# An adaLN block with ProbSparse attention and a soft mixture of experts: the stages of both batches interleaved, and the buffers laid out anew

## The reference

```python
h = layernorm(x) * (1 + ca) + sa                       # per batch
q, k, v = split_heads(h @ Wq + bq), ...(Wk, bk), ...(Wv, bv)
scores = einsum('bhqd,bhkd->bhqk', q, k) * scale
sparsity = scores.max(-1) - scores.mean(-1)
_, top_idx = top_k(sparsity, U)                        # per batch and head
out_sel = softmax(scores_of(q[top_idx], k)) @ v
out = zeros_like(q).at[top_idx].set(out_sel)           # other rows stay zero
x = x + ga * (out @ Wo + bo)
h = layernorm(x) * (1 + cb) + sb
x = x + gb * soft_moe(h)    # rmsnorm, dispatch softmax over tokens, gelu experts, combine softmax
```

## Time and profile before

| | |
|---|---|
| median of 3 runs | 1887.63 us (1884.67 to 1888.17) |
| profiled execution | 1887.74 us, span 1886.0 us, granted TensorE clock 0.913 on average |
| TensorE busy | 1544.0 us, 82% (weight loads 842.5) |
| VectorE busy | 1222.6 us, 65%; 589.6 of it the 512 row maxima L917 |
| ScalarE busy | 1012.3 us, 54% |
| GpSimd busy | 262.8 us, 14% |
| stages of batch 0 | projections 44.10 to 128.70; maxima to 431.20; selection to 485.70; attention to 624.24; output projection and norms to 680; experts and mix to 965.20 |
| stages of batch 1 | projections 965.20 to 1048.60; maxima to 1350.10; selection to 1404.40; attention to 1542.50; the rest to 1886.0 |

### The profile page before, as it was taken

How to read it: one execution, slowest core, us unless ns; L and a number is a source line. 1 busy time by engine, 2 the same in 40 slices (tenths; PEclk the granted TensorE clock), 3 DMA queues, 4 the chain that set the end, 5 groups by cost and what they waited for, 6 DMA issues and landing times.

```text
span 1886.0 us, 29389 instructions
## 1 busy us (share of the span) xinstructions
PE 1544.0 (82%) x8114; PEld 842.5 (45%) x8114; DVE 1222.6 (65%) x3085; ACT 1012.3 (54%) x1342; POOL 262.8 (14%) x294
## 2 busy tenths in 40 slices
PE   2779999993799658898988799999649974979989
PEld 1342222222455423787854222222225533448878
DVE  3539999998777466223134699999977838642211
ACT  1338888882466232433523688888526643333343
POOL 1440000001044200210015100000103440011100
PEclk7879999995799879899998899999859987989989
DMA  9431111121011300243014211112111112004410
GB/s 256 142 97 34 50 34 50 36 65 51 18 53 52 94 1 0 70 148 114 28 47 138 51 43 41 46 38 56 35 44 45 53 41 79 0 14 151 142 39 31
DMA packets 91776, 119.08 MB, mean 63 GB/s; under 512 B 21346, under 2 KB 77378, under 8 KB 91204
## 3 DMA queue, kind: packets, MB, share of 16 engines
q1 hardware_dynamic: 88644, 117.73, 20.9%
q0 software_dynamic: 3072, 0.66, 0.4%
HBM read 93.54 MB, written 24.78 MB: 63 GB/s over the span
## 4 chain that ended last, share of the span: by engine, by line
PE 40%; DVE 34%; issue 13%; ACT 3%; DMA 3%; POOL 3%; SPq 2%; DVEq 1%; PEld 0%; ACTq 0%; PEldq 0%; POOLq 0%
DVE work_area L917 23%; PE psum L1517 6%; PE psum L1564 6%; PE psum L1372 4%; PE psum L1487 4%; PE psum L1395 4%; PE psum L1539 3%; PE psum L1384 3%; PE psum L1525 3%; DVE work_area L947 2%; POOL work_area L486 2%; PE psum L1556 2%; DMA work_area<-q_parts 1%; PE psum L1264 1%; DVE work_area L851 1%
## 5 line engine op out<-in xcount | busy, mean ns | idle before, releaser
L917 DVE CUSTOM_DVE_ANT_0 work_area<-psum,work_area 128x1024 f32<-128x1024 f32 x512 | 589.6, 1220 | 47.6 <-ACT work_area L630 42.7
L630 ACT ACTIVATE work_area<-psum 128x1024 f32<-128x1024 f32 x512 | 510.9, 1027 | 91.2 <-DVE work_area L917 30.6
L1300 PE MATMUL psum<-work_area 96*128 96x512 bf16 x1024 | 311.8, 386 | 47.6 <-DVE work_area L917 7.2
L1290 PE MATMUL psum<-work_area 96*128 96x512 bf16 x1024 | 310.2, 385 | 20.0 <-DMA work_area<-q_parts 14.6
L651 ACT ACTIVATE work_area<-psum 128x614 f32<-128x614 f32 x256 | 164.0, 681 | 80.5 <-PE psum L1384 80.4
L1300 PEld LDWEIGHTS psum<-work_area 96*128 96x128 bf16 x1024 | 64.6, 98 | 266.8 <-DVE work_area L917 249.2
L1290 PEld LDWEIGHTS psum<-work_area 96*128 96x128 bf16 x1024 | 89.7, 98 | 168.8 <-ACT work_area L630 58.2
L1517 PE MATMUL psum<-xn,work_area 128*128 128x257 f32 x512 | 118.8, 391 | 6.3 <-ACT work_area L703 6.3
L990 DVE TENSOR_SCALAR big_area<-iota,rank 128x308 bf16<-128x308 f16 x512 | 122.2, 317 | 0.0
L1487 PE MATMUL psum<-slots_T,work_area 128*128 128x512 f32 x256 | 119.6, 613 | 0.1
L534 POOL DMA_INDIRECT heads_out<-work_area x96 | 99.4, 1036 | 141.2 <-DVE work_area L1019 120.5
(11 more groups left out here) (227 smaller groups left out, 1918.2 us busy)
## 6 DMA issues: line engine op xcount, KB each, us to landing
work_area<-in_L_ffn_w_dram SPq DMA_DIRECT2D x32, 1024.0 KB, 5.2
work_area<-q_parts SPq DMA_DIRECT2D x192, 64.0 KB
k_parts<-work_area SPq DMA_DIRECT2D x24, 384.0 KB, 3.2
work_area<-k_parts SPq DMA_DIRECT2D x32, 192.8 KB
q_parts<-work_area SPq DMA_DIRECT2D x16, 384.0 KB, 2.5
work_area<-q_parts SPq DMA_DIRECT2D x16, 384.0 KB, 5.1
work_area<-k_parts SPq DMA_DIRECT2D x32, 192.0 KB
work_area<-k_parts SPq DMA_DIRECT2D x32, 128.5 KB
```

The costliest lines, as they stand in the source:

```text
L630: s.activation(SC[:, t % 4], PS[:, 2 * (n % 2):2 * (n % 2) + 2].rearrange("p a n -> p (a n)"), ACT.Relu).then_inc(relu_done, 1)
L917: v.tensor_tensor_reduce(SC[:, t % 4], PS[:, 4 + 2 * (t % 2):6 + 2 * (t % 2)].rearrange("p a n -> p (a n)"), SC[:, t % 4], 1.0, -3.0e38, A ...
L1290: last = mm(PS[:, 2 * (n % 2) + k], QS1[par][0:TERMS, t * P:(t + 1) * P], KS[par][0:TERMS, k * 512:(k + 1) * 512], start=True, stop=True)
L1300: last = mm(PS[:, 4 + 2 * (t % 2) + k], QS1[par][0:TERMS, t * P:(t + 1) * P], KS[par][0:TERMS, K1 + k * 512:K1 + (k + 1) * 512], start=Tru ...
```

## The change

The stages of the two batches no longer follow one another: on TensorE, VectorE and ScalarE the order is now projections 0, maxima 0, selection 0 with the projection units of batch 1 in it, attention 0, maxima 1, selection 1 with the value tiles of batch 1 in it, output projection 0, attention 1, experts 0, output projection 1, experts 1. Mean, variance and deviation of batch 1's tokens are formed ahead of maxima 0.

`share(q)` gives the units that round q of the first search carries: one, and two in rounds 3, 7, 11 and 15. TensorE does them behind the natural-order transposes of the round; VectorE does the residual and the cast for `share(q - 1)` between its compares and the wait for the count. GpSimd normalises batch 1's tokens itself. With this go:

- a third residual buffer and a third group buffer `QG` for queries; units use three PSUM banks, natural-order transposes one;
- the next group is turned right behind the first unit of a group; differences are made behind units 0 and 10; the mean key comes at unit 13 (`MEAN_AT`), both in batch 0 as in batch 1;
- keys and queries of the maxima (`KS`, `QS1`) get an area of their own at the end of the working area, which they share with the parts `SPL`, so the first heads are loaded once all parts have been written out; the attention's keys `K2S` lie over the scratch of the search, so their paddings are set behind the ranks (`pads`);
- the SP queue's order, and the search written out instead of looped.

The diff, cut to its core:

```diff
+    MEAN_AT = 13
+    opens = lambda u: u == 0 or UNITS[u - 1][0] < UNITS[u][0]
+    share = lambda q: range(q * NU // ROUNDS, (q + 1) * NU // ROUNDS)
...
         a = Area(work)
-        KS = [a.take([2056], BF16) for _ in range(2)]
-        QS1 = [a.take([L], BF16) for _ in range(2)]
...
-        R1 = a.take([2, GW])
...
+        R1 = a.take([3, GW])
...
+        a = Area(work, parts_at)
+        SPL = a.take([SLOTS, 3, GW], BF16)
+        a = Area(work, parts_at)
+        KS = [a.take([2056], BF16) for _ in range(2)]
+        QS1 = [a.take([L], BF16) for _ in range(2)]
...
+            def first_heads(b):
                 for k in range(SLOTS):
                     sp.wait_ge(parts_out[k], 16 * (NU // SLOTS) * (b + 1))
+                sp.wait_ge(kbar_out, 32 * (b + 1))
+                for par in range(2):
+                    head_to_sbuf(b, 0, par)
...
+            for u in range(NU):
+                parts_to_dram(0, u)
+            first_heads(0)
+            other_heads(0)
+            for g in range(3):
+                queries_to_sbuf(0, g)
+            for u in range(NU):
+                parts_to_dram(1, u)
+                if u == share(G + 1)[-1]:
+                    queries_to_sbuf(0, 3)
+            attention_keys(0)
+            first_heads(1)
+            other_heads(1)
+            for g in range(NG):
+                queries_to_sbuf(1, g)
+            sp.wait_ge(base_ready, 2 * NT + B * H * NT)
+            heads_to_sbuf(0, 0, NT // 4)
+            attention_keys(1)
...
+            def third_part(b, u):
+                pool.wait_ge(part2_ready, b * NU + u + 1)
+                g.tensor_tensor(SPL[:, u % SLOTS, 2], R1[:, u % 3], SPL[:, u % SLOTS, 1], ALU.subtract).then_inc(parts_ready, 1)
+                if u % 10 == 0:
+                    hdiff(b, u // 10)
...
+            def pads(b):
+
                 g.memset(Vh, 0.0).then_inc(pads_ready, 1)
                 g.memset(OS, 1.0).then_inc(pads_ready, 1)
+                pool.wait_ge(rank_ready, b + 1)
+                pool.wait_ge(nm_ready, b + 1)
                 for k in range(2):
                     last = g.memset(K2S[k], 1.0)
...
+            def experts(b):
+
+                for k in range(2):
+                    act.wait_ge(scattered[k], B * PAIRS * CH * 16)
...
+            def residual(b, u):
+
+                g, kind, cc = UNITS[u]
+                dve.wait_ge(part1_ready, b * NU + u + 1)
+                if u > 2:
+                    dve.wait_ge(parts_ready, b * NU + u - 2)
...
+            def split_units(b, units):
+
+                for u in units:
+                    if u == MEAN_AT:
+                        mean_hidden(b)
+                    residual(b, u)
                     if u:
-                        second_part(u - 1)
-                    if u == NU - 2:
-                        mean_key_parts()
-                second_part(NU - 1)
+                        second_part(b, u - 1)
+                    if u == MEAN_AT + 1:
+                        mean_key_parts(b)
...
+                for q in range(ROUNDS):
+                    for k in range(3):
+                        last = v.tensor_scalar(cmpo[:, k], spTf, cand.bitcast(F32)[:, k:k + 1], 0.0, ALU.is_ge, ALU.add, accum_out=cnt[:, k:k + 1])
+                    last.then_inc(cnt_ready, 1)
+                    if b == 0 and q:
+                        split_units(1, share(q - 1))
+                    dve.wait_ge(tot_ready, b * ROUNDS + q + 1)
...
                 v.tensor_scalar(masks[:, 1], spT, thr, None, ALU.is_equal).then_inc(masks_ready, 1)
+                if b == 0:
+                    split_units(1, share(ROUNDS - 1))
+                    second_part(1, NU - 1)
...
+                last.then_inc(qk_ready, 1)
+                if g < NG - 1 and opens(u):
+                    turn_tokens(b, g + 1)
+                if u == MEAN_AT:
+                    mean_key(b)
...
                 for q in range(ROUNDS):
                     pe.wait_ge(cnt_ready, b * ROUNDS + q + 1)
-                    mm(PS[:, 1, 0:3], same_head[:], cnt[:, 0:3], start=True, stop=True).then_inc(tot_ready, 1)
-                    natural(q)
+                    mm(PS[:, 7, 0:3], same_head[:], cnt[:, 0:3], start=True, stop=True).then_inc(tot_ready, 1)
+                    natural(b, q)
+                    if b == 0:
+                        for u in share(q):
+                            unit(1, u)
+                    else:
+                        value_tile(1, q)
...
+            attend(0)
+            maxima(1)
+            select(1)
+            pe.wait_ge(v_copied, B * NT)
+            pe.wait_ge(qn_ready, B * NT)
+            project_heads(0)
+            attend(1)
+            experts(0)
```

624 lines of the change are left out of this document (337 added, 287 removed).

## The result

The changed kernel takes 1820.57 us (median of 4 runs, 1814.84 to 1823.53) against 1887.9 us (four runs of the kernel before; the 1887.63 further up is of three); the ratio is 0.9641 (95% interval 0.9613 to 0.9669), 67 us or 3.6% less. The forecast was 1818 us.

A forecast was written before the change was run, and what follows sets the result against it. The prediction took the serial order of the two batches as the bound, with batch 1's projections (83.4 us) and the threshold searches as thin stages. Terms summed to -69.3 us from 1887.7, so 1818 us; range 1800 to 1840.

The forecast's parts named there:

- (a): Batch 1's projection stage leaves the serial path, its units and value tiles going into the two searches: -83.4 us.
- They just fit: Loads of batch 1's first two heads: issued 17 us before attention 0 ends, such loads taking 14.2 us.
- (b): First search grows by carrying batch 1's 20 units: 79.0 us against 42.7, +36 us.
- The step that rested on a memset's row: First search: VectorE's integer shift waits 0.94 us for the rest of GpSimd's third part, as beside a memset.
- The bound without a waiting shift: First search if no shift waits: rounds of 3.4 and 5.2 us, search growing by about 24 us.
- (c): Batch 0's projections get shorter, mainly since a third residual buffer ends the wait for GpSimd: -11 us, bounds 4 and 15.
- (d): Hand-overs: attention to output projection -10.6 us for batch 0, -4.6 for batch 1; maxima 1 starting at full clock -1.5.
- (e): Attention of batch 0 starts later, as GpSimd's key-buffer memsets come after the ranks and VectorE waits for them: +3.8 us.
- (f): Second search carries one value tile per round: +2 us, bounds 0 and +6.
- The signs that hang on (c): Expected in the new profile: first matmul of the maxima at 117 to 118 us, ranks of batch 0 at about 509.
- the low-clock case: Rival: TensorE stays at 1.2 GHz in the first search, which grows by 52 us; 1834 us in all, chance 0.19.
- a round with the whole way of a unit: Rival, first search: nothing overlaps, each unit adds 6.4 us, search 167 us; 1906 us in all, chance 0.05.

The follow-up runs named there:

- casts early: Changed kernel with each unit's second part (cast) moved from behind the next residual to the start of the next round, ahead of the compares; ratio 0.9579.

## Why the prediction was right

The time (1818 forecast, 1820.6 measured) and the sum (-69.3; -67 by medians, -72.9 by the profiled executions) agree, but partly since misses offset each other.

- **(a), -83.4.** The stretch is gone. "They just fit" was half right: the loads landed in time, but the 18 transfers held up the last head's keys, and TensorE fell to the low clock: some 2.5 of the attention's +6.9 us. Moving them proved dearer (8.1 and 6.6 us). An attention that changed its length was named as a sign of being wrong, and in this it was one.
- **(b), +36.** Measured +34.5 in the profiled execution, which is the fastest; in the other profile of the changed kernel it is +39.3, so the agreement is in part that of this one execution. Rounds with one unit 3.96 us (forecast 4.1), with two 5.4 to 6.3 (5.7), the shift 1.08 us (1.1). The step that rested on a memset's row, that the shift would wait for a subtraction too, is confirmed by leaving the subtraction out (0.16 us) and by moving it (0.16 us). The round with the mean key took 10.1 us, 4.4 more than my 5.7 (forecast 5). What I lacked were the two steps that wait for the differences (rounds of 6.0 us, twice). What paid for them was the tail: units 18 and 19 between masks and ranks cost 0.5 us, not 4.3 (9.6 us against 9.1), also because the prefix sums ran at the high clock there; in the second profile the tail is 3.8 us longer than before. The bound without a waiting shift was put at 3.4 us, though its four figures add up to 3.5; with the subtraction left out most rounds took 3.0 to 3.5.
- **(c), -11.** The term that was mis-sized: -5.2. My 48 us from the first residual to the last third part were 54.9 (52.37 to 107.26). The openings cost 6.3 us of waits (I took 7). The mean key cost a wait of 2.35 us, which I had only as 2 us of work, and two of the three waits were followed by matmuls at the low clock, 5 us longer in all than at the full one, for which I had 1 us. TensorE's waits for the differences, which I let go, are indeed gone. The third buffer alone gave 5.8 us in batch 0 of the kernel before, with those waits still there, so what else was changed in this stage gave nothing net.
- **(d), -16.7.** Output projections of both batches -9.6 and -11.8, experts of batch 0 +4.5: -16.9, for which I had -15.2. The first sum came 3.6 us after the ranks (3.3 allowed), and ScalarE's first step in the experts 8.3 us after the attention, as forecast. The other 1.5 us, maxima that start at full clock, show in projections and maxima 1: -84.8, against -84.9 with (a).
- **(e), +3.8.** The first gather came 9.0 us after the ranks, 4.6 before: +4.4.
- **(f), +2.** Wrong in sign: -5.2. The +2 had no working of its own; the row's 1.95 us of TensorE work in a round of 2.43 said that nothing would be added, and nearly nothing was. Two things were missed. The memsets of the earlier trace rows no longer hold the shift in the second search (two shifts of 0.73 and 1.61 us are 0.16 now; the search takes 39.3 us instead of 42.9, and why three more rounds got 0.5 us shorter is not shown). And the value tiles keep TensorE at its high clock, so that the prefix sums behind the search take 1.8 us instead of 3.1 to 3.4.
- **Luck.** (c) and the attention's end cost 8 us more than forecast, and (f), which I had with the wrong sign, gave back 7. The signs that hang on (c) came late: first matmul of the maxima at 123.5 us (117 to 118 forecast), ranks at 515.2 (509).
- **The rivals.** The clock went to 0.90 over the selection, so the low-clock case did not come; nor did the one of a round with the whole way of a unit. The rule of the Trainium skill (SBUF — State Buffer, Who interferes with whom) that a tensor_scalar in a two-port mode waits for a running GpSimd instruction to its end is what the traces show for the shift: 1.08 us beside a 1.15 us subtraction. Single units of the search ran at the low clock (3.0 to 3.4 us instead of 1.9), and the four executions, 1814.84 to 1823.53 us, have mean clocks from 0.944 down to 0.936 in the same order. By the Trainium skill (TensorE: Matmul & The Clock Gate, the part on psum-queue depth-cycling) such going back and forth comes with short idle spells between groups of matmuls; the trace agrees as far as the single slow units go, and the four executions lie within 8.7 us.

Where the 83.4 us went: 62.4 were units (965.3 to the first value tile at 1027.66), 14.0 value tiles, and 7.0 the wait for the loads. The tiles now cost next to nothing and the loads little. The units take 49.7 us in a block (the third buffer by itself saves 4.6 of the difference), of which the search hides 10 us net and, with the casts early, about 23.

## What to carry to other kernels

When work is put into a latency-bound chain of another engine, look not only at busy times but at what runs beside each small step: here 0.92 of the 1.53 us by which a round grew was one VectorE step of 0.16 us that waited for a GpSimd instruction of 1.15 us begun just before it, and moving the start of that instruction to where operations follow that don't wait, the three compares of the next round, gave 11.5 us. Filling the idle spells of TensorE can pay twice, since what follows directly may run at the high clock: behind a second search with value tiles in it, it did in every profile; behind the first, where TensorE waits 2.35 us first, only in some executions. Loads that are moved off the critical path still compete in their queues with the loads of the stage that hides them, early, late or spread.

## What the runs showed of the hardware that was not expected

- The integer shift, the small integer additions and the casts on VectorE wait for a running GpSimd subtraction to its end, and the steps then one by one for each that follows it (1.08, 1.18 and 1.19 us in a row). Copies last as long as the memsets beside them (six in 4.05 us, 1.38 without). Compares with a sum, the small reduction, and instructions that read PSUM kept their lengths beside GpSimd (0.48, 0.16 and 0.75 us).
- A memset of 2048 bf16 columns takes 1.76 us on VectorE, no less than on GpSimd; over half as many 32-bit elements the stage behind it starts 1.7 us sooner.
- 18 transfers (the keys and queries of two heads) issued ahead of a head's keys delay that head by 8.9 us, spread by threes they still cost 7.0 us in all, behind the last keys 1.5 us and a low clock.
- Chips differ: with the same instructions the attention took 138 to 146 us on some and 152 to 160 on others. The exponentials last 0.68 us each on both kinds; on the slower kind ScalarE starts some of them over 1 us later once per head (idle for 2.45 us instead of 0.84) and TensorE waits 0.6 to 0.8 us for it. Why is not shown.
